# Moving the maximum units of an attention kernel forward by one query tile and interleaving the last of them

## The reference

```python
xn = _layernorm(x, ln_scale, ln_bias)
q = (xn @ Wq).reshape(b, n, HEADS, d).transpose(0, 2, 1, 3)
kv = xn @ Wkv
k, v = jnp.split(kv, 2, axis=-1)
...
q = _layernorm(q, qn_scale, qn_bias)
k = _layernorm(k, kn_scale, kn_bias)
dots = jnp.einsum('bghqd,bgkd->bghqk', qg, k) * scale
attn = jax.nn.softmax(dots, axis=-1)
out = jnp.einsum('bghqk,bgkd->bghqd', attn, v)
return out @ Wout
```

## Time and profile before

| | us |
|---|---|
| median of the three timed runs | 905.59 |
| lowest and highest of them | 902.62, 906.96 |
| the profiled execution: its time | 907.61 |
| the profiled execution: its span, first to last instruction | 905.8 |
| TensorE busy in the span | 843.1 (93%) |
| VectorE, GpSimd, ScalarE busy | 612.4, 564.8, 465.3 |
| mean granted TensorE clock | 0.966 |

### The profile page before, as it was taken

How to read it: one execution, slowest core, us unless ns; L and a number is a source line. 1 busy time by engine, 2 the same in 40 slices (tenths; PEclk the granted TensorE clock), 3 DMA queues, 4 the chain that set the end, 5 groups by cost and what they waited for, 6 DMA issues and landing times. The chain is left out here.

```text
span 905.8 us, 13476 instructions
## 1 busy us (share of the span) xinstructions
PE 843.1 (93%) x4860; PEld 447.0 (49%) x4860; DVE 612.4 (68%) x1040; ACT 465.3 (51%) x838; POOL 564.8 (62%) x369
## 2 busy tenths in 40 slices
PE   4897999999999999989799999999999964999998
PEld 3444444544444445554444444444445422567665
DVE  5667678777787776267668777777777546156772
ACT  2674555555556655566455555555555623344521
POOL 2553687778878887535478688868886943046510
PEclk9998999999999999999799999999999985999999
DMA  6000000000000000000000000000000002000001
GB/s 166 1 1 1 1 1 2 1 2 1 2 1 1 2 1 2 0 1 2 1 1 2 1 1 1 1 2 1 1 1 1 1 4 70 25 1 1 1 1 47
DMA packets 49597, 7.99 MB, mean 9 GB/s; under 512 B 42486, under 2 KB 47994, under 8 KB 49530
## 3 DMA queue, kind: packets, MB, share of 16 engines
q1 hardware_dynamic: 48666, 6.99, 4.9%
q10 hardware_dynamic: 864, 0.13, 0.1%
HBM read 5.92 MB, written 1.05 MB: 8 GB/s over the span
## 5 line engine op out<-in xcount | busy, mean ns | idle before, releaser
L430 POOL TENSOR_TENSOR space<-space 128x1024 f32<-128x1024 f32 x160 | 380.4, 2378 | 39.5 <-ACT space L804 21.3
L1057 DVE TENSOR_REDUCE part<-psum 128x2 f32<-128x1024 f32 x256 | 313.1, 1223 | 124.8 <-PE psum L550 121.4
L804 ACT ACTIVATE space<-psum 128x512 f32<-128x512 f32 x512 | 264.6, 603 | 162.1 <-PE psum L570 153.9
L585 PE MATMUL psum<-space,vb 128*64 128x512 f32 x1024 | 249.4, 609 | 0.0
L550 PE MATMUL psum<-kh,qh 64*128 64x512 f32 x512 | 128.8, 500 | 12.4 <-DVE part L1057 12.2
L435 POOL TENSOR_TENSOR space<-space 128x1024 f32<-128x1024 f32 x30 | 71.6, 2388 | 98.9 <-DVE space L1073 98.9
L550 PEld LDWEIGHTS psum<-kh,qh 64*128 64x128 f32 x512 | 48.2, 185 | 145.4 <-DVE part L1057 109.7
L585 PEld LDWEIGHTS psum<-space,vb 128*64 128x64 f32 x1024 | 62.8, 137 | 108.3 <-issue 72.8
L570 PE MATMUL psum<-qh,kh 64*128 64x512 f32 x512 | 104.0, 402 | 1.0 <-DMA ql<-nmx 1.0
L570 PE MATMUL psum<-qh,kl 64*128 64x512 f32 x512 | 103.2, 397 | 0.0
L570 PE MATMUL psum<-ql,kh 64*128 64x512 f32 x512 | 102.8, 396 | 0.0
(11 more groups left out here) (160 smaller groups left out, 881.3 us busy)
## 6 DMA issues: line engine op xcount, KB each, us to landing
ql<-nmx SPq DMA_DIRECT2D x256, 0.5 KB, 2.0
w1s<-in_L_ffn_W SPq DMA_DIRECT2D x4, 256.0 KB, 2.7
w2s<-in_L_ffn_W SPq DMA_DIRECT2D x4, 256.0 KB
out<-x SPq DMA_DIRECT2D x4, 256.0 KB, 2.6
x<-in_L_attn_x SPq DMA_DIRECT2D x2, 256.0 KB, 4.4
wproj<-in_L_attn_Wq SPq DMA_DIRECT2D x1, 512.0 KB, 6.8
x<-in_L_attn_x SPq DMA_DIRECT2D x1, 512.0 KB, 7.7
wout<-in_L_attn_Wout SPq DMA_DIRECT2D x1, 512.0 KB, 6.9
```

The lines of the kernel that those rows point to most:

```text
L430: pool.tensor_tensor(to, pt[0] if u == 1 else to, pt[u], ALU.add)\
L585: last = pe.matmul(outp[rows(h), :], vb[:, place(m)[1], kt, :], pt[kt][:, h, :], start=(kt == 0), stop=(kt == TILES - 1))
L804: act.activation(pt[kt][:, h, :], key_scores[kt % 2][h], ACT.Exp).then_inc(exp_made, 1)
L1057: dve.tensor_reduce(to[:, half, :], scores.rearrange("p (h k) -> p h k", h=2), AX_X, ALU.max, negate=True)\
```

## The change

The table of work is the same; only its order on TensorE and VectorE differs. Unit 0 now stands before `norms` of tile 4. All units of the produced tiles are one place further: a tile is `norms`, an odd unit, transposes, `folded`, an even unit. Behind the last tile, TensorE alternates: transposes of tile 6, unit 9, score tile 0, unit 10, score tile 1, transposes of tile 7, unit 11. VectorE follows in the same order of units. The TensorE attention loop starts at phase 6, since units 10 and 11 have moved into `produce`. Lines behind the edits move: L1057 is L1063 after, L1049 is L1055.

```diff
-                for ph in range(LAG, end):
+                for ph in range(LAG + 1, end):
...
+            def early_unit(b, w):
+
+                unit_scores(SLOTS * b + w // 8, w % 8)
+
             def produce(b):
 
+                early_unit(b, 0)
                 for j in range(T, TILES):
                     norms(b, j)
-                    unit_scores(SLOTS * b, 2 * (j - T))
+                    early_unit(b, 2 * (j - T) + 1)
                     turn_queries(b, j - 2)
                     folded(b, j)
-                    unit_scores(SLOTS * b, 2 * (j - T) + 1)
+                    early_unit(b, 2 * (j - T) + 2)
                 turn_queries(b, TILES - 2)
-                unit_scores(SLOTS * b + 1, 0)
-                unit_scores(SLOTS * b + 1, 1)
+                early_unit(b, 9)
                 tile_scores(SLOTS * b, 0)
+                early_unit(b, 10)
                 tile_scores(SLOTS * b, 1)
                 turn_queries(b, TILES - 1)
+                early_unit(b, 11)
...
+            def early_largest(b, w):
+
+                largest(SLOTS * b + w // 8, w % 8)
+
             def produce(b):
 
+                early_largest(b, 0)
                 for j in range(T, TILES):
                     sum_queries(b, j)
-                    largest(SLOTS * b, 2 * (j - T))
+                    early_largest(b, 2 * (j - T) + 1)
                     low_queries(b, j - 2)
-                    largest(SLOTS * b, 2 * (j - T) + 1)
-                largest(SLOTS * b + 1, 0)
+                    early_largest(b, 2 * (j - T) + 2)
+                early_largest(b, 9)
                 low_queries(b, TILES - 2)
-                largest(SLOTS * b + 1, 1)
-                largest(SLOTS * b + 1, 2)
+                early_largest(b, 10)
+                early_largest(b, 11)
                 low_queries(b, TILES - 1)
-                largest(SLOTS * b + 1, 3)
```

## The result

| | median us | runs | lowest, highest | ratio to before (95% interval) |
|---|---|---|---|---|
| before | 905.38 | 4 | 902.62, 906.96 | |
| changed | 896.27 | 4 | 894.57, 900.37 | 0.9899 (0.9869 to 0.9929) |
| changed, measured again beside other kernels | 894.4 | 6 | 892.75, 898.91 | 0.9887 (0.9866 to 0.9907) |

The changed kernel is about 1% faster, 9 to 11 us. The profiled execution of the changed kernel took 900.37 (span 898.6), 4.1 above its median; that of before took 907.61, 2.2 above its.

A forecast was written before the change was run, and what follows sets the result against it. TensorE was taken to bound the kernel. The profiled 907.61 us + 2.7 (heads) - 2 x 5.7 (tails) = 898.9, and with 0.5 for occasional clock falls about 899.3; the range was 896.0 to 904.8.

The forecast's parts named there:

- What bounds: Whole kernel: TensorE, busy 843.1 of 905.8 us; time won before unit 14 is kept to the attention's end.
- The head: Start of each transition: unit 0 ahead of `norms` of tile 4 costs 2.2 us in batch 0, 0.5 in batch 1.
- the slower rival: Head and loop: the clock falls behind unit 0's wait, losing up to 3.2 or 6.5 us, up to 910.8; chance 0.03.
- The loop: Production loop: costs nothing, square to square stays 5.91 us.
- the cover: Loop: idle time of VectorE (0.97 us) and TensorE (0.33) hides a 0.3 us delay; without it 2.4 us for eight tiles.
- The tail: Behind the last produced tile: VectorE's chain brings unit 14 from 94.62 to 88.90 us, 5.7 us gained per tail.
- Clock and order: Tail: about 4 of the 5.7 us gained are clock, the order alone is worth 1.7.
- the bound beside it: Changed tail reckoned with the slow clock's values throughout: unit 14 at 91.60 us, a gain of 3.0.
- The clock rule: Tail: if transposes don't count as PE-busy, those of tile 7 wouldn't hold the clock; the sum would be 904.3 us.
- The sum: Whole kernel: profiled 907.61 plus heads 2.7 less two tails of 5.7, plus 0.5 for clock falls: about 899.3 us.
- The clock falls as before: Rival, tails: the low clock stays, so each gains only 3.0 us, total 904.3; chance 0.23.
- Order alone: Rival, tails: timed runs before may already have the high clock; only 0.7 us gained, 902 to 905; chance 0.10.

The follow-up runs named there:

- c1: The changed kernel itself, unaltered, measured again beside the follow-up kernels: 894.4 us, ratio 0.9887 to before.
- e3: The kernel before with 16 needless matmuls per batch in TensorE's idle pieces of the tail, order untouched: 895.86 us, ratio 0.9879.
- e5: The changed kernel with 9 needless matmuls per batch in the tail's longest idle pieces: 895.38 us, ratio 0.9903.
- e9: The kernel before with needless matmuls ahead of units 11 and 12 only, 11 per batch: 900.76 us, ratio 0.9943.
- e1: The changed kernel without the interleaving, units still one place later, score tile 0 behind unit 10: 900.78 us, ratio 0.9929.

## Why the prediction held, point by point

- **What bounds.** Right: TensorE is full behind unit 14, and 312.81 us lie between the marks before and after, to the hundredth.
- **The head.** 2.2 us predicted for batch 0, 2.4 measured (c1): unit 0 starts 0.35 us behind the copy's end and not 0.05. Batch 1: 0.6 for 0.5 (the first square behind the head 5.13 us behind the transposes of tile 1 and not 4.51). The price that the sum left to the slower rival did come in the profiled execution: the clock fell behind the idle piece (0.61 at 56 to 60 us), and the transition of batch 0 took 44.31 us against 42.80 in c1, where it didn't fall. 1.5 us, not the 3.2 of that rival: the fall lasted 3.4 us, not 6.5 (in stretches of 1 us the clock is 0.50 from 57 to 60, and 0.94 and 0.85 in those beside them), and half of 3.4 is 1.7.
- **The loop.** Right in batch 0: 77.61 - 71.70 = 5.91 us from square to square, as in the earlier trace rows. In batch 1 one of the three distances is 6.09 (418.65 to 424.74), so the cover wasn't quite whole there; with the head that makes 0.8 us for batch 1, by which its transition gains 5.4 and not 6.2.

```profile
71.70 1.02 ACT L768 ACTIVATE space<-psum 128x1024 f32<-128x1024 f32 x1 [1.10 <-PE psum L454]
...
77.61 1.03 ACT L768 ACTIVATE space<-psum 128x1024 f32<-128x1024 f32 x1 [1.04 <-PE psum L454]
```

- **The tail.** The chain was right link by link and 0.5 us too long over 14.2: units 9 to 14 were put 2.76, 4.57, 7.33, 9.14, 11.90 and 14.20 us behind unit 8, and came 2.58, 4.40, 6.99, 8.81, 11.40 and 13.71 behind it. The step from a merge to the low part and the one from the low part to the next maximum were each taken too long by 0.1, three times. Gain 6.2 a tail instead of 5.7.
- **Clock and order.** Mechanism right, shares a little off: 4 us clock and 1.7 order were estimated; e3, e5 and the old tail give 3.5 to 3.9 and 2.3 to 2.7. The 4 doesn't follow from the bound beside it, which gives 5.7 - 3.0 = 2.7. It needs the slow rows added up: 2.4 for units 12 to 14, 0.5 for the transposes and 1.2 for the score tiles (2.64 against 1.48 at full clock, 94.96 to 96.44), 4.1 in all.
- **The clock rule.** By the Trainium skill's page "TensorE: Matmul & The Clock Gate", section "Part 4: PE-mode transpose", transposes don't count as busy in the same way, and so the tail might have gone low. The trace doesn't bear out that result: the clock stayed at 1.00 in the stretch of 84 to 88 us, which holds nearly all of the transposes of tile 7 (87.03), and in 88 to 92 behind them, where TensorE is busy 2.46 of 4.00, and likewise in both tails of after and of c1. Whether transposes count is still open.
- **The sum.** The forecast is 3 us above the first median and 5 above the second, which lies outside the range; that the first lies inside is partly luck. Two things were missed. The forecast took the sum from the profiled 907.61 and set it against medians, with the reason that it "is for the kernel after, at high clock". But that execution also held low stretches that the change doesn't touch (28 to 32 and 738 to 769 us); the median run likely has fewer (its mean clock is higher, but it has no trace). Taken from the median, the same terms give 905.6 + 2.7 - 11.4 + 0.5 = 897.4. And the change is worth more than its terms: by before and c1, 3.80 and 5.35 us in the two transitions (42.80 for 46.60, 40.28 for 45.63) and 1.1 at the end of the span, 10.2 in all, where the sum has 8.7 and nothing at the end. 905.4 - 10.2 = 895.2 lies between the two medians. (898.9 + 0.5 is 899.4 and not 899.3.)
- **Rivals.** "The clock falls as before" (904.3) is refuted in four tails of two traces. "Order alone" is refuted: no timed run of before was under 902, and filling its idle pieces alone brought it to 895.9, so the clock isn't high in the median run of before.

## What to carry to other kernels

Where TensorE waits in short pieces for another engine, count what the low clock does to the work behind the pieces; here it was more than half of what a tail gained (3.5 to 3.9 of 6.2 us), and sixteen needless matmuls per batch bought as much as the reordering. To tell the two apart, fill the idle pieces with harmless work and leave the order alone. An interleaving helps only if what it puts between has nothing left to wait for: first move the producer of the slow wait forward, then interleave. And take a sum from a profiled execution to the median with the difference that the kernel before shows between them.

## What the runs showed of the chip that I hadn't expected

- 32 added matmuls made a 905 us kernel 9.6 us faster (e3), 7.4 us of it in the two tails of the trace.
- One order, run twice in one execution, kept the clock in one batch and lost it in the other (e9, tails of 16.01 and 18.47 us; e1, 13.93 and 15.47).
- Executions of one kernel on one chip fall into groups by mean granted clock: e1 took 894.5 to 896.0 at 0.979 to 0.981 and 900.6 to 902.0 at 0.973, c1 892.8 at 0.983 and 898.9 at 0.975. The spread of the timings in this study is in large part that clock, and one place of it is the stretch near 30 us, worth some 3 us.
- The end of the span, in code that the change doesn't touch, is 1.1 us shorter in all nine traces of the new order than in the four of the old one. The cause is open.
